# Attention scores as float32 products in quarters of the array instead of packed halves

## The chip, the cores and the metric

The kernel runs on one core of one Trainium2 chip. The metric is the device time of one execution in microseconds. Three executions of the kernel before gave 1820.46, 1821.09 and 1821.55 us, median 1821.09 us. The engines are TensorE (PE in the rows, its weight loads PEld), VectorE (DVE), ScalarE (ACT), GpSimd (POOL) and the DMA queues, here those that SyncE fills (SP).

## What is computed

Input is `x` of shape (8, 512, 128). Four layers follow, each as `x = x + layernorm(layer(layernorm(x)))`: a linear attention with a feed-forward part (stage `pf` in the kernel), a rotary attention with a causal mask and a choice of two of eight experts (`rope` and `mo`), a context attention (`ctx`), and a gated expert network (`sw`). The change touches the two softmax attentions. Both have 16 heads of 8 channels and 512 tokens in each of 8 samples. The rotary one:

```python
q_in = rope(x)                                  # keys from it too, values from x
q, k, v = (inp @ W.T + b).reshape(B, S, 16, 8)
scores = einsum('bqhd,bkhd->bhqk', q, k) * 8 ** -0.5
scores = where(causal, scores, -inf)
out = einsum('bhqk,bkhd->bqhd', softmax(scores), v) @ Wo.T + bo
```

The context attention has no mask and adds one term for all heads, from 16 further channels:

```python
ctx = X @ We.T                                  # 16 channels a token
scores = einsum('bhqd,bhkd->bhqk', Q, K) * 8 ** -0.5 + 0.1 * einsum('bqe,bke->bqk', ctx, ctx)[:, None]
```

So a score of the rotary layer sums 8 channels, one of the context layer 24.

## The kernel before

`attention_layer` holds both attentions (`causal` tells them apart). A sample's 16 heads go in 4 groups of `GH = 4`; the queries of a head are 4 tiles of 128 tokens. A softmax needs the largest score of each query first, then the exponentials, and it is computed in two products:

- **Scores** (`score`, L1310, into `s` banks): queries in the rows of the result, keys along 512 columns. VectorE takes the largest of each row (`largest`, L1176, `nm`), negated. In the rotary layer a tile needs only the keys up to its own (128, 256, 384 or 512 columns), and a bf16 product adds the mask (L1313).
- **By key** (`scores_by_key`, L1657, into `st` banks): keys in the rows, queries along the columns, with the negated largest score as one more channel, the guard. ScalarE writes `exp` of it to `probs` (L1554, 1024 columns at a time); in the rotary layer GpSimd zeroes the future (L1419).
- **Values** (`weigh_values`, L1673, into `out`): for each key block the four heads of a group go to the four column quarters of the array, each as a 128 x 32 float32 product.

The operands of the first two are stacks of channels, `qst` and `kst`, in fp32r. Each channel stands in them as a high and a low half, in three rows (high by low, low by high, high by high), which makes 24 rows in the rotary layer and 72 in the context layer, in a stack of 96; the guard takes rows 96 and 97. A product by the full array then gives the float32 result in one pass. The halves are made by GpSimd (`halves_of`, L1106 and L1108, `halves_of_context`), written to DRAM by `store_halves` (L1034) and loaded per group by `load_stack` (L1047, L1050). The guard is cut in two halves on VectorE (`cut_guard`, L1185, L1188), transposed (L1193) and goes to DRAM and back (L1054, L1062) for each group.

The loop of a layer runs over rounds `b` (samples) and 32 steps `h` in each, eight to a group. In a round TensorE scores the group two ahead, makes the products by key of the present group and the values of the group behind (in two lots, at the steps 3 and 7 of a group). Into the steps are put the side products of the samples before and after: turning the tokens, the projections q, k, v and c, turning the output (`o0`, `o1`, `oT`) and projecting it (`wo`). The score banks are a ring, `SR = 3`: `vacated` makes a product wait for whoever reads what the bank held three uses earlier, for a score the reduction (semaphore `s_used`). In the context layer side products use the ring too; in the rotary layer they have a bank of their own (`side`). Two pairs of `st` banks alternate. ScalarE copies the output bank after every second group (L1561), twice a sample.

The first group's scores of sample 0 are made by the stage before, in banks lent by it (`pf_dve`; `mo_side` and `mo_lp`). The stage `pf` uses parts of the attention buffers as its own memory (`room`).

## Time and profile before

| what | us |
|---|---|
| median of three executions | 1821.09 |
| profiled execution, its own time | 1818.61 |
| its span, first to last instruction | 1816.9 |
| TensorE busy | 1527.4 (84%) |
| VectorE busy | 1249.6 (69%) |
| ScalarE busy | 1027.1 (57%) |
| GpSimd busy | 793.7 (44%) |
| first layer (`pf`) | about 0 to 370 |
| rotary attention loop | about 373 to 756 |
| experts (`mo`) | about 760 to 930 |
| context attention loop | about 934 to 1401 |
| last layer (`sw`) | to the end |

Busy time of an engine over the whole span mixes stages with different limits, so the table of stretches below is read stage by stage. A record of a TensorE product is longer than the time that the array streams, as the next one starts before it ends; where a group of products follows without a gap, the difference of starts is what one costs. "x8" behind a row of a timeline counts records.

### The profile page before, as it was taken

What the parts mean: (1) busy time and instruction counts of PE and PEld (TensorE: products, weight loads), DVE (VectorE), ACT (ScalarE), POOL (GpSimd) and SP (SyncE); (2) the same over time, 40 slices, a digit from 0 to 9 for tenths busy, and PEclk for the clock granted to TensorE, in tenths of its full rate; (3) what the DMA queues carried; (4) which work ended last, traced back from release to release, by engine and by line L of the source; (5) the groups of instructions that cost most, each with busy time, mean ns of one, the idle gap of its engine ahead of it and who ended that gap; (6) DMA issues with size and microseconds to landing.
All of it is one profiled execution on the core that took longest, in us unless ns stands there. A gap on an engine that the chain in (4) does not pass through costs nothing. (4 is left out here: it accounts for less than half of the span.)

```text
span 1816.9 us, 26731 instructions
## 1 busy us (share of the span) xinstructions
PE 1527.4 (84%) x8757; PEld 964.7 (53%) x8757; DVE 1249.6 (69%) x3212; ACT 1027.1 (57%) x1749; POOL 793.7 (44%) x902
## 2 busy tenths in 40 slices
PE   3788888689999999588769999999997686999980
PEld 1444555466666666343335545555553565777770
DVE  1656667467777777267777778777882574888875
ACT  2444555335666655424636677677675554777762
POOL 2244534435555544324741111222001576688875
PEclk8888989759999999788868999999998698999995
DMA  6800000212222221000244444443530022344415
GB/s 214 278 1 1 1 1 1 61 60 78 69 74 72 70 73 35 4 14 1 72 107 122 109 110 121 120 120 92 131 72 1 32 68 90 117 126 136 126 55 139
DMA packets 96201, 144.30 MB, mean 79 GB/s; under 512 B 31266, under 2 KB 59939, under 8 KB 91952
## 3 DMA queue, kind: packets, MB, share of 16 engines
q1 hardware_dynamic: 91072, 134.11, 26.5%
q0 software_dynamic: 4992, 8.48, 1.4%
q8 instruction: 71, 1.16, 0.3%
q14 instruction: 66, 0.54, 0.1%
HBM read 104.19 MB, written 57.48 MB: 89 GB/s over the span
## 5 line engine op out<-in xcount | busy, mean ns | idle before, releaser
L1176 DVE TENSOR_REDUCE ctx_nm<-ctx_s 128x1 f32<-128x512 f32 x496 | 320.0, 681 | 87.4 <-PE ctx_s L1310 86.6
L1176 DVE TENSOR_REDUCE rope_nm<-rope_s 128x1 f32<-128x128 f32 x496 | 223.5, 481 | 83.0 <-PE rope_s L1313 80.7
L1554 ACT ACTIVATE rope_probs<-rope_st 128x1024 f32<-128x1024 f32 (+1 forms) x256 | 172.2, 702 | 139.1 <-PE rope_st L1657 137.9
L1554 ACT ACTIVATE ctx_probs<-ctx_st 128x1024 f32<-128x1024 f32 x192 | 190.3, 1023 | 87.6 <-PE ctx_st L1657 84.1
L1310 PE MATMUL ctx_s<-att_kst,att_qst 96*128 96x512 f32 x496 | 210.9, 459 | 19.4 <-DVE ctx_nm L1176 8.4
L1310 PE MATMUL rope_s<-att_kst,att_qst 96*128 96x128 f32 x496 | 179.0, 392 | 8.8 <-PEq L120 5.5
L1657 PE MATMUL ctx_st<-att_qst,att_kst 98*128 98x512 f32 x512 | 164.7, 404 | 2.4 <-ACT ctx_probs L1554 1.5
L1419 POOL TENSOR_SCALAR_AFFINE_SELECT rope_probs<-rope_probs 128x256 f32<-128x256 f32 x256 | 98.1, 408 | 156.1 <-ACT rope_probs L1554 155.6
L1310 PEld LDWEIGHTS ctx_s<-att_kst,att_qst 96*128 96x128 f32 x496 | 95.8, 193 | 127.3 <-DVE ctx_nm L1176 51.0
L1657 PE MATMUL rope_st<-att_qst,att_kst 98*128 98x512 f32 (+3 forms) x512 | 141.2, 360 | 3.9 <-ACT rope_probs L1554 3.9
L2930 DVE TENSOR_TENSOR sw_hl<-sw_hf,sw_hh 128x512 fp32r<-128x512 f32 x124 | 128.5, 1037 | 0.1
L2924 DVE TENSOR_TENSOR sw_hf<-sw_silu,sw_u 128x512 f32<-128x512 f32 x124 | 84.7, 683 | 62.8 <-ACT sw_silu L2682 58.1
L2682 ACT ACTIVATE sw_silu<-sw_g 128x512 f32<-128x512 f32 x124 | 74.3, 599 | 92.4 <-PE sw_g L110 91.9
L1673 PE MATMUL ctx_out<-ctx_probs,att_vaug 128*32 128x512 f32 x768 | 122.5, 598 | 0.0
L1310 PEld LDWEIGHTS rope_s<-att_kst,att_qst 96*128 96x128 f32 x496 | 100.5, 203 | 37.3 <-issue 22.3
L2782 POOL DMA_INDIRECT sw_ys<-sw_yo,sw_xin x92 | 104.2, 1132 | 29.1 <-issue 24.0
L1313 PE MATMUL rope_s<-rope_maskb,rope_identb 128*128 128x128 bf16 x496 | 116.5, 239 | 0.0
L1657 PEld LDWEIGHTS ctx_st<-att_qst,att_kst 98*128 98x128 f32 x512 | 98.3, 194 | 24.4 <-issue 4.6
L1657 PEld LDWEIGHTS rope_st<-att_qst,att_kst 98*128 98x128 f32 x512 | 92.1, 200 | 14.6 <-ACT rope_probs L1554 5.9
L2761 POOL TENSOR_TENSOR sw_wl<-sw_raw,sw_wh 128x1536 fp32r<-128x1536 f32 x24 | 84.1, 3503 | 34.8 <-ACT sw_wh L2660 34.8
L1673 PE MATMUL rope_out<-rope_probs,att_vaug 128*32 128x512 f32 (+3 forms) x1024 | 84.1, 448 | 3.0 <-POOL rope_probs L1419 3.0
L2688 ACT ACTIVATE sw_hh<-sw_hf 128x512 fp32r<-128x512 f32 x124 | 77.3, 624 | 5.5 <-DVE sw_hf L2924 5.5
(429 smaller groups left out, 3467.1 us busy)
## 6 DMA issues: line engine op xcount, KB each, us to landing
sw_raw<-in_L_ffn_all SPq DMA_DIRECT2D x24, 768.0 KB, 4.4
sw_xs<-in_pad SPq DMA_DIRECT2D x65, 260.0 KB, 9.5
rope_halves<-att_qk SPq DMA_DIRECT2D x24, 512.0 KB
ctx_halves<-att_qk SPq DMA_DIRECT2D x24, 512.0 KB, 5.7
att_qst<-ctx_contexts SPq DMA_DIRECT2D x32, 384.0 KB
att_kst<-ctx_contexts SPq DMA_DIRECT2D x32, 384.0 KB
att_qst<-rope_halves SPq DMA_DIRECT2D x32, 192.0 KB
att_kst<-rope_halves SPq DMA_DIRECT2D x32, 192.0 KB
```

The lines of the kernel that those rows point to most:

```text
L1176: nc.vector.tensor_reduce(nm[:, g, j * T + t:j * T + t + 1], bank("s", b, n)[:, 0:keys], AXX, ALU.max, negate=True).then_inc(s_used, 1)
L1310: last = nc.tensor.matmul(out[:, 0:keys], qst[0:KS, g, j, t * P:(t + 1) * P], kst[0:KS, g, j, 0:keys], start=True, stop=not causal)
L1313: last = nc.tensor.matmul(out[:, keys - P:keys], identb[:], maskb[:], start=False, stop=True)
L1419: last = nc.gpsimd.affine_select(blocks, blocks, [[0, 2], [1, P]], compare_op=ALU.is_ge, fill=0.0, base=0, channel_multiplier=-1)
L1554: nc.scalar.activation(prob(n // GH % 2, n % GH)[:, u * units[0]:u * units[0] + units[u]], st_bank[u][:, 0:units[u]], ACT.Exp, scale=SCALE ...
L1657: last = nc.tensor.matmul(st_bank[u][:, lo:lo + width[c]], kst[:, g, j, c * P:(c + 1) * P], qst[:, g, j, S - width[c]:S], start=True, stop ...
L1673: last = nc.tensor.matmul(o_bank[32 * j:32 * j + 32, S - width[c]:S], vaug[g // 2][:, s, c, j, :], prob(s, j)[:, at(c):at(c) + width[c]], ...
L2688: nc.scalar.activation(hh[m % RING][:], hf[m % 3][:], ACT.Copy).then_inc(hh_ready, 1)
L2761: nc.gpsimd.tensor_tensor(wl[s % WR][:], raw[s % 2][:], wh[s % WR][:].bitcast(F32), ALU.subtract).then_inc(wl_ready, 1)
L2782: nc.gpsimd.indirect_dma_start(ys[:, :], bass.IndirectOffsetOnAxis(ap=where_to, axis=0), yo[j % YR][:, t, :], None, bounds_check=2 * B * S ...
L2924: nc.vector.tensor_tensor(hf[m % 3][:], silu[m % 2][:], u_bank[m % 2][:], ALU.mult).then_inc(hf_ready, 1)
L2930: nc.vector.tensor_tensor(hl[m % RING][:], hf[m % 3][:], hh[m % RING][:].bitcast(F32), ALU.subtract).then_inc(hl_ready, 1)
```

## The change

Each head's channels are now stored once, as plain float32, and the four heads of a group stand in the four quarters of the partitions (`QUARTER = 32`): rows 0 to 7 of a quarter are the channels, in the context layer rows 8 to 23 the context, and row 31 (`GUARD`) the guard, as one float32 number against ones in `kst`. A product takes 31 rows (scores) or 32 (by key) of a quarter of the array's rows and all 128 columns. All code for halves goes. The scores of a pair (two heads, one query tile) and the products by key of the other two heads (one key block) make a step:

```diff
-            def score(b, g, j, t):
-                n = (g * GH + j) * T + t
+            def scores(b, pair):
 ...
-                vacated("s", b, n)
-                keys = P * (t + 1) if causal else S
-                out = bank("s", b, n)
-                last = nc.tensor.matmul(out[:, 0:keys], qst[0:KS, g, j, t * P:(t + 1) * P], kst[0:KS, g, j, 0:keys],
-                                        start=True, stop=not causal)
-                if causal:
-                    last = nc.tensor.matmul(out[:, keys - P:keys], identb[:], maskb[:], start=False, stop=True)
-                last.then_inc(s_ready, 1)
+                two = (2 * pair, 2 * pair + 1)
+                g = pair // PAIRS
+                for n in two:
+                    vacated("s", b, n)
+                    j, t = scored(n % (GH * T))
+                    keys = P * (t + 1) if causal else S
+                    rows = slice(QUARTER * j, QUARTER * j + GUARD)
+                    last = nc.tensor.matmul(bank("s", b, n)[:, 0:keys], qst[rows, b % 2, g, t * P:(t + 1) * P], kst[rows, b % 2, g, 0:keys],
+                                            start=True, stop=not causal)
+                    if not causal:
+                        last.then_inc(s_ready, 1)
+            def hide_future(b, pair):
+                for n in (2 * pair, 2 * pair + 1):
+                    keys = P * (scored(n % (GH * T))[1] + 1)
+                    nc.tensor.matmul(bank("s", b, n)[:, keys - P:keys], identb[:], maskb[:], start=False, stop=True).then_inc(s_ready, 1)
```

`scored` gives the heads 2 and 3 in even steps and 0 and 1 in odd ones; the products by key take the others:

```diff
-            def scores_by_key(b, g, j, u):
+            def scores_by_key(b, g, i):
+                m = (b * NG + g) * PAIRS + i
+                if i == 0:
+                    pe.wait_ge(m_loaded[g % 2], (b * NG // 2 + g // 2 + 1) * 16)
+                if m >= 2:
+                    pe.wait_ge(p_ready, m - 1)
+                c, half = i // 2, i % 2
+                for k in range(2):
+                    rows = slice(QUARTER * (2 * half + k), QUARTER * (2 * half + k + 1))
+                    last = nc.tensor.matmul(st_bank[half][:, k, 0:width[c]], kst[rows, b % 2, g, c * P:(c + 1) * P],
+                                            qst[rows, b % 2, g, S - width[c]:S], start=True, stop=True)
 ...
                     ahead, behind = group(b, g + 2), group(b, g - 1)
                     if within(ahead[0]) and not lead(ahead):
-                        score(*ahead, j, 2 * u)
+                        scores(ahead[0], ahead[1] * PAIRS + i)
                     now = keys_step(b, h)
                     if now:
-                        scores_by_key(now[0], now[1] // 8, j, u)
-                    if within(ahead[0]) and not lead(ahead):
-                        score(*ahead, j, 2 * u + 1)
+                        scores_by_key(*now)
+                    if within(ahead[0]) and not lead(ahead) and causal:
+                        hide_future(ahead[0], ahead[1] * PAIRS + i)
```

In the rotary layer the columns of a step now fall over the group, for scores and products by key alike: 512, 512, 384, 384, 256, 256, 128, 128. The banks stay eight: three score banks, four by key (the rotary side bank goes there, and its side products into the ring), one for the output. Storing and loading are by sample:

```diff
-            def load_stack(b, g, side_tile, side):
 ...
+            def load_stacks(b):
+                if causal and b == 0:
+                    sp.wait_ge(init, 4)
+                sp.wait_ge(stored, (b + 1) * NS)
+                for side, st in enumerate((qst, kst)):
+                    src = parts[b, side].rearrange("(d g j) t -> j d g t", g=NG, j=GH)
+                    for j in range(GH):
+                        row = QUARTER * j
+                        sp.dma_start(st[row:row + DH, b % 2], src[j]).then_inc(stacks_loaded[b % 2], 16)
+                        if not causal:
+                            sp.dma_start(st[row + DH:row + DH + CE, b % 2], contexts[b, side].unsqueeze(1).broadcast_to([CE, NG, S])).then_inc(stacks_loaded[b % 2], 16)
```

VectorE transposes `nm` itself (`turn_guard`), with no cut. GpSimd clears both stacks and sets the value buffers once at the start of `pf` (`prepare`) instead of in its rounds and at the loop's start, and `pf` gets buffers of its own in place of `room`.

TensorE's order in the context loop, before, with the number of the score bank and of the by-key bank:

```order
L1657 MATMUL ctx_st1<-att_qst,att_kst 128x512 x2
L1310 MATMUL ctx_s1<-att_kst,att_qst 128x512
L1287 MATMUL ctx_s2<-att_yT,att_wk 128x512
L1310 MATMUL ctx_s0<-att_kst,att_qst 128x512
L1657 MATMUL ctx_st0<-att_qst,att_kst 128x512 x2
L1310 MATMUL ctx_s1<-att_kst,att_qst 128x512
L1310 MATMUL ctx_s2<-att_kst,att_qst 128x512
L1657 MATMUL ctx_st1<-att_qst,att_kst 128x512 x2
L1310 MATMUL ctx_s0<-att_kst,att_qst 128x512
```

The same loop after the change:

```order
L1280 MATMUL ctx_s1<-att_kst,att_qst 128x512
L1280 MATMUL ctx_s2<-att_kst,att_qst 128x512
L1600 MATMUL ctx_st1<-att_qst,att_kst 128x512 x2
L1280 MATMUL ctx_s0<-att_kst,att_qst 128x512
L1280 MATMUL ctx_s1<-att_kst,att_qst 128x512
L1600 MATMUL ctx_st0<-att_qst,att_kst 128x512 x2
L1572 MATMUL ctx_s2<-ident,mo_we 128x128 x4
L1280 MATMUL ctx_s0<-att_kst,att_qst 128x512
L1280 MATMUL ctx_s1<-att_kst,att_qst 128x512
```

One score stood on either side of the two products by key; now both stand ahead of them, and the second takes the bank that the first one of the step before had (`s1` after `s1`, two rows apart).

TensorE's order in the rotary loop, before:

```order
L1310 MATMUL rope_s1<-att_kst,att_qst 128x128
L1313 MATMUL rope_s1<-rope_maskb,rope_identb 128x128
L1657 MATMUL rope_st0<-att_qst,att_kst 128x512
L1657 MATMUL rope_st0<-att_qst,att_kst 128x384
L1657 MATMUL rope_st0<-att_qst,att_kst 128x128
L1310 MATMUL rope_s2<-att_kst,att_qst 128x256
L1313 MATMUL rope_s2<-rope_maskb,rope_identb 128x128
```

And after the change:

```order
L1280 MATMUL rope_s1<-att_kst,att_qst 128x256
L1280 MATMUL rope_s2<-att_kst,att_qst 128x256
L1600 MATMUL rope_st0<-att_qst,att_kst 128x256 x2
L1288 MATMUL rope_s1<-rope_maskb,rope_identb 128x128
L1288 MATMUL rope_s2<-rope_maskb,rope_identb 128x128
L1280 MATMUL rope_s0<-att_kst,att_qst 128x256
L1280 MATMUL rope_s1<-att_kst,att_qst 128x256
L1600 MATMUL rope_st1<-att_qst,att_kst 128x256 x2
```

The mask, on all rows and columns of the array, stood right behind its score; now both masks of a step stand behind the step's four products.

## Rows read from the trace of the kernel before

**Rows 1.** Table of stretches: from:to, length, busy us by engine, PEclk, DMA

```profile
365.00:420.00 55.00, 49.18 (x256) 34.67 (x259) 35.15 (x91) 19.91 (x32) 23.92 (x45) 0.68 0.24 74
...
420.00:735.00 315.00, 306.46 (x2437) 210.75 (x2436) 243.05 (x695) 191.29 (x322) 164.69 (x320) 1.00 0.21 64
985.00:1370.00 385.00, 374.25 (x1979) 201.81 (x1978) 308.78 (x689) 272.08 (x335) 63.28 (x85) 1.00 0.44 111
907.00:927.00 20.00, 10.97 (x16) 4.53 (x16) 15.49 (x41) 6.58 (x17) 11.56 (x10) 0.50 0.62 120
```

**Rows 2.** Timeline of ScalarE: start us, length us, the copies of the output bank

```profile
514.40 0.60 ACT L1561 ACTIVATE rope_oe<-rope_out 128x512 f32<-128x512 f32 x1 [0.74 <-PE rope_out L1673]
...
561.48 0.60 ACT L1561 ACTIVATE rope_oe<-rope_out 128x512 f32<-128x512 f32 x1 [0.73 <-PE rope_out L1673]
...
1104.70 0.60 ACT L1561 ACTIVATE mo_we<-ctx_out 128x512 f32<-128x512 f32 x1 [1.09 <-PE ctx_out L1673]
...
1162.28 0.60 ACT L1561 ACTIVATE mo_we<-ctx_out 128x512 f32<-128x512 f32 x1 [1.10 <-PE ctx_out L1673]
```

**Rows 3.** Timeline of TensorE in the context loop, scores and values

```profile
1108.99 0.39 PE L1310 MATMUL ctx_s<-att_kst,att_qst 96*128 96x512 f32 x1
1109.31 1.92 PE L1673 MATMUL ctx_out<-ctx_probs,att_vaug 128*32 128x512 f32 x16
...
1111.98 0.63 PE L1310 MATMUL ctx_s<-att_kst,att_qst 96*128 96x512 f32 x2
```

**Rows 4.** Timeline of TensorE in the first stage, two products in column quarters

```profile
51.53 0.62 PE L316 MATMUL pf_act<-pf_sqq,pf_hsel 128*32 128x512 f32 x1
51.54 0.62 PE L317 MATMUL pf_act<-pf_sqk,pf_hsel 128*32 128x512 f32 x1
51.98 0.59 PE L316 MATMUL pf_act<-pf_sqq,pf_hsel 128*32 128x512 f32 x1
51.99 0.59 PE L317 MATMUL pf_act<-pf_sqk,pf_hsel 128*32 128x512 f32 x1
```

**Rows 5.** Timeline of TensorE in the rotary loop, around values

```profile
560.39 0.23 PE L1313 MATMUL rope_s<-rope_maskb,rope_identb 128*128 128x128 bf16 x1
560.55 0.86 PE L1673 MATMUL rope_out<-rope_probs,att_vaug 128*32 128x256 f32 x16
561.34 0.33 PE L1310 MATMUL rope_s<-att_kst,att_qst 96*128 96x128 f32 x1
```

**Rows 6.** Timeline of the context loop, hand-overs between TensorE and VectorE

```profile
1107.49 0.65 DVE L1176 TENSOR_REDUCE ctx_nm<-ctx_s 128x1 f32<-128x512 f32 x1
...
1108.19 0.50 PE L1310 MATMUL ctx_s<-att_kst,att_qst 96*128 96x512 f32 x1 [0.19 <-DVE ctx_nm L1176]
...
1111.17 0.50 PE L1310 MATMUL ctx_s<-att_kst,att_qst 96*128 96x512 f32 x1
...
1111.70 4.39 DVE L1176 TENSOR_REDUCE ctx_nm<-ctx_s 128x1 f32<-128x512 f32 x7 [1.03 <-PE ctx_s L1310]
```

**Rows 7.** Groups by shape, rotary loop: xcount, busy us, mean ns, idle before

```profile
L1176 DVE TENSOR_REDUCE rope_nm<-rope_s 128x1 f32<-128x512 f32 x109 | 72.8, 668 | 0.0
...
L1176 DVE TENSOR_REDUCE rope_nm<-rope_s 128x1 f32<-128x128 f32 x108 | 30.7, 284 | 31.4 <-PE rope_s L1313 31.1
```

**Rows 8.** Timeline of TensorE in the context loop, two side products

```profile
1099.78 1.13 PE L1644 MATMUL ctx_s<-ctx_wo,ctx_oT 128*128 128x128 f32 x8
...
1121.57 0.63 PE L1628 MATMUL ctx_s<-ident,mo_we 128*128 128x128 f32 x4 [0.28 <-DVE ctx_nm L1176]
```

**Rows 9.** Timeline of TensorE in the expert stage, first group's scores

```profile
912.63 0.80 PE L1310 MATMUL mo_side<-att_kst,att_qst 96*128 96x512 f32 x1 [0.19 <-DVE ctx_nm L1176]
...
914.21 0.79 PE L1310 MATMUL mo_side<-att_kst,att_qst 96*128 96x512 f32 x1 [0.19 <-DVE ctx_nm L1176]
```

**Rows 10.** GpSimd in the first stage: timeline row, then a group by shape

```profile
26.57 1.26 POOL L487 TENSOR_TENSOR att_qk<-pf_y,pf_bo 128x512 f32<-128x512 f32 x1 [18.07 <-DMA pf_be<-in_L_attn_be]
...
L1122 POOL MEMSET att_kst<- 96x2048 f32 x4 | 7.2, 1804 | 0.0
```

More of the change, by code:

```diff
@@ L246, in _ @@
                 sp.dma_start(dst[:], src).then_inc(signal, 16)
-            behind.store_halves(0)
-            behind.fill_stacks()
+            behind.store_parts(0)
+            behind.load_stacks(0)
+            behind.store_parts(1)
+            behind.load_stacks(1)
             behind.store_guard(0, 0)
@@ L461, in _ @@
                     behind.project_values(1)
-                    for n in range(GH * T):
-                        behind.score(0, 0, n // T, n % T)
+                    for pair in range(GH * T // 2):
+                        behind.scores(0, pair)
+                        behind.hide_future(0, pair)
         @block.gpsimd
@@ L515, in _ @@
             behind.set_half()
+            behind.prepare()
             for b in rounds:
@@ L530, in _ @@
                     behind.turn(1, 0)
-                    pool.wait_ge(r_ready, B)
-                    behind.halves_of(0, 0)
-                    behind.halves_of(0, 1)
                 if within(f2):
@@ L727, in _ @@
                     if b == B + 2 + n // (GH * T // 2):
-                        behind.largest(0, 0, n // T, n % T)
-            for step in range(3):
-                behind.cut_guard(0, 0, step)
+                        behind.largest(0, n)
+            behind.turn_guard(0, 0)
         @block.scalar
@@ L994, in attention_layer, with scored @@
         rounds = range(-1, B + 1)
-        lent_bank, ring, side, lent = [], [], [], []
+        def scored(n):
+            i, k = n // 2, n % 2
+            return 2 * (1 - i % 2) + k, T - 1 - i // 2 if causal else i // 2
+        lent_bank, ring, lent = [], [], []
         for c in range(LEAD):
@@ L1004, in attention_layer @@
             for h in range(STEPS):
-                to, tg = group(b, h // 8 + 2)
+                to, tg = group(b, h // PAIRS + 2)
                 if within(to) and not lead((to, tg)):
-                    ring += [("s", to, tg * GH * T + h % 8 * 2 + k) for k in range(2)]
+                    ring += [("s", to, tg * GH * T + h % PAIRS * 2 + k) for k in range(2)]
                 for name, step in AT.items():
@@ L1010, in attention_layer @@
                     if step == h and within(own) and (name in OUTPUTS or own >= LEAD):
-                        (side if SIDE else ring).append((name, own, 0))
-        spot = {use: (uses, n) for uses in (ring, side, lent) for n, use in enumerate(uses)}
-        assert len(spot) == len(ring) + len(side) + len(lent) == B * (GH * NG * T + len(AT))
+                        ring.append((name, own, 0))
+        spot = {use: (uses, n) for uses in (ring, lent) for n, use in enumerate(uses)}
+        assert len(spot) == len(ring) + len(lent) == B * (GH * NG * T + len(AT))
         def banks(name, b, k=0):
             uses, n = spot[name, b, k]
-            return uses, n, lent_bank if uses is lent else side_bank if uses is side else s_bank
+            return uses, n, lent_bank if uses is lent else s_bank
         def bank(name, b, k=0):
@@ L1023, in keys_step @@
         def keys_step(b, h):
[L1025 to L1029 removed]
+            if b * STEPS + h < PAIRS:
+                return (0, 0, b * STEPS + h + PAIRS) if -PAIRS <= b * STEPS + h < 0 else None
+            return (b, h // PAIRS, h % PAIRS) if within(b) else None
+        s_bank = []
         def on_sync(sp):
[L1032 to L1050 removed]
@@ L1324, in attention_layer @@
         s_bank += [ps(f"s{k}", 512) for k in range(SR)]
-        side_bank += [ps(f"side{k}", 512) for k in range(SIDE)]
-        st_bank = [ps("st0", 1024), ps("st1", 512 if causal else 1024)]
+        st_bank = [main.enter_context(nc.psum_tensor(layer + f"st{k}", [P, 2, 512], F32)) for k in range(2)]
         o_bank = ps("out", 512)
@@ L1445, in _ @@
                     now = keys_step(b, h)
-                    if causal and now and h % 2 == 1:
-                        hide_future(now[0], now[1] // 2)
+                    if causal and now:
+                        hide_future(*now)
                     if within(c) and c >= LEAD:
@@ L1452, in _ @@
                             turn(c, h - TURN)
-                        for k, name in enumerate("qk"):
-                            if h == AT[name] + 1:
-                                halves_of(c, k)
-                        if not causal and h == AT["c"] + 1:
-                            halves_of_context(c, 0)
-                            halves_of_context(c, 1)
                     if within(a):
@@ L1589, in _ @@
                     if now:
-                        exponentials(now[0], now[1] // 2, h % 2)
+                        exponentials(*now)
                     if within(c) and c >= LEAD:
@@ L1622, in _ @@
         def _(pe):
-            vacated, turn_tokens, turn_rotated, project, project_values, project_context, score = on_tensor(pe)
+            vacated, turn_tokens, turn_rotated, project, project_values, project_context, scores, hide_future = on_tensor(pe)
             def turn_out(a, hf):
@@ L2092, in _ @@
                             project_ahead(c, (b - first - 2) * T + t)
-                    for n in SCORED.get((b, t), []):
-                        next_layer.score(0, 0, n // T, n % T)
+                    for pair in SCORED.get((b, t), []):
+                        next_layer.scores(0, pair)
                     if ahead and t == 0:
```

328 lines of the change are left out of this document (118 added, 210 removed).

## The prediction

> **What bounds the kernel now.** I first read the table of stretches [rows 1]. In the loop of the rotary attention (420 to 735 us) TensorE is busy 306.5 of 315 us, in the loop of the context attention (985 to 1370 us) 374 of 385 us, both at a granted clock of 1.00, which is 2.4 GHz. VectorE follows with 243 and 309 us. So TensorE sets both loops, VectorE is close behind in the second, and everything that the change takes from GpSimd and the DMA queues lies under cover there. The copy of the output bank by ScalarE comes twice a sample, so every second one gives the time of a sample: 561.48 - 514.40 = 47.1 us (rotary), 1162.28 - 1104.70 = 57.6 us (context) [rows 2]. These two periods are what the change alters. A steady sample has all its scoring; groups are scored two ahead and the first one by the stage before, so each loop scores 31 groups of 4 to a sample, 7.75 samples.
>
> **Products.** A packed product of 512 columns is one record, and dense ones start 0.63 - 0.39 = 0.24, in longer runs 0.23 us apart [rows 3]. A float32 product is two records: 16 records for four heads and two key blocks take 1.92 us, of which 0.16 is the tail of the last; so 2 x 4 products take 1.76 us, and four products in four column quarters run in 0.86 us, the time of one [rows 3]. That they overlap across quarters, though each has two records, shows in the first stage: two products of L316 and L317 begin 0.01 us apart, and their second records 0.45 us later, again 0.01 apart [rows 4]. The queue does not wait for the second record of one quarter before it starts another. The trace has columns in quarters, not rows. I take rows in quarters to overlap as well (nearest row), and keep a serial array, 4 x 0.86 = 3.44 us, as the other end.
> A step of the context loop was 4 x 0.23 = 0.93 us of streaming; it becomes 0.86 us if all four products start together. That saving, 0.07 x 32 = 2.2 us a sample, is all there is to win on the array.
>
> **Changes of tiling.** Between the full array and the quarters of the value products the stream stops: the mask product of 560.39 streams until 560.46 (0.23 less the tail of 0.16) and the value products begin at 560.55; they end at 561.25, and the scores begin at 561.34 [rows 5]. That is 0.09 us each way. Behind values of 512 columns (end 1111.07) the score of 1111.17 has a record of 0.50 instead of 0.39 [rows 3, 6], 0.2 in all. I take 0.14. The trace has no change from row quarters to full; bounds 0 and 0.3.
> In the context loop this adds two changes for each of nine side products a sample, in the rotary loop two for each step, since the mask stays a product on the full array.
>
> **The wait that decides.** The ring of scores keeps 3 banks. A step asks for two of them; the second one is the bank of the first product of the step before. Its wait stands ahead of both products by key in TensorE's queue. Hand-overs: a reduction that ends at 1108.14 lets a product start at 1108.19 (0.05), whose record is 0.50 instead of 0.39 long, since its weights were not loaded ahead (0.10) [rows 6]; a product that ends at 1111.67 is reduced from 1111.70 (0.04), and seven reductions in a row take 4.39 us, 0.62 apart [rows 6], each 0.67 long [rows 7]. From the start of a first product to the start of the next step's second one: 0.86 + 0.16 + 0.04 + 0.67 + 0.05 + 0.10 = 1.9 us. Before, the same round trip was 0.23 + 0.16 + 0.04 + 0.67 + 0.15 = 1.25 us and had three dense products of 0.23 and the products by key to hide in. The longer product, not the number of reductions, makes the difference.
> Half a group of the context loop, from a free array at 0: step 0 starts all four at 0. Step 1: first at 0.86 (its quarter is then free), second at 1.9, by key at 1.9. Step 2: first at 1.9 + 0.86 = 2.76, second at 3.1 (its bank's reduction is the third in VectorE's row), by key 3.1. Step 3: first 4.0, second 2.76 + 1.9 = 4.65, by key 4.65, end 5.5. Then the value products: 0.14 + 1.72 + 0.14. Sum 7.5 us, eight times a sample: 60.0. The nine side products: three of 512 columns at 0.86, two of eight records at 1.13 - 0.16 = 0.97 less overlap, 0.9 [rows 8], four turns of four records, 0.63 - 0.16 = 0.47 with the start, 0.44 [rows 8], together 6.1, and 9 x 0.28 = 2.5 for tiling. **Context sample 68.7 us, +11.1.**
> Half a group of the rotary loop: columns fall 512, 512, 384, 384, and the scores are only ready behind the mask. From one mask to the next step's second product: 0.23 (mask record) + 0.04 + reduction + 0.05 + 0.10 = 0.42 + 0.67 for 512 columns, 0.42 + 0.28 for 128 [rows 7]; I put 0.55 and 0.42 between. First half: mask at 0.86 + 0.14 = 1.0; then +1.09 + 1.0 = 3.1; +1.09 + 0.78 = 4.95; +0.97 + 0.78 = 6.7; two masks, tiling and values (0.86 + 0.64) give 8.6. Second half (256, 256, 128, 128): 0.57, +0.84 + 0.57 = 1.98, +0.84 + 0.36 = 3.2, +0.70 + 0.36 = 4.25, and 1.0 behind them: 5.25. A group 13.85, a sample 55.4. Side products 2 x 0.86 + 2 x 0.9 + 5 x 0.44 = 5.7, whose tiling is already counted. **Rotary sample 61.1 us, +14.0.**
> Over 7.75 samples: +86 and +108.
>
> **Fronts.** The first group of the context loop is scored inside the expert stage, at a granted clock of 0.50 (1.2 GHz) [rows 1] and with two lent banks: a pair each 914.21 - 912.63 = 1.58 us [rows 9]. Now a product is 1.71 us, and the second bank comes back after 1.71 + 0.25 + 0.04 + 0.62 + 0.68 + 0.15 = 3.4 us; eight pairs +14.6 us, of which other VectorE work hides perhaps a third: +10. The rotary front has falling columns and masks: +8. The first round of each loop still runs at the low clock (0.68 on the mean of 365 to 420 us [rows 1]), where the longer products cost double: +5.
> **Under cover.** GpSimd loses the halves and the clearing; in both loops it waits more than it works. It now clears the stacks at its start, four memsets of 1.8 us (96 x 2048 took 1.80 [rows 10]) and the value buffers, some 2.3 us, until about 16.5 us; it sat idle 18.07 us up to 26.57 for a load [rows 10], and TensorE's first projection waits for a load as well: +1 (0 to +5). Two cuts a group (VectorE, 0.3 us) go, on an engine that waits here. A sample's stacks are loaded at once, behind one guard and ahead of the next in the queue, with fewer bytes; there is most of a group (14 us and more) for it. 0, at most +2 a sample if a guard is late. The first stage no longer borrows memory: 0 to -5.
> **Sum** against the profiled execution, 1818.6 us (span 1816.9 and 1.7 around it; the median of the runs is 1821.1): 1818.6 + 86 + 108 + 10 + 8 + 5 + 1 = 2036.6, say **2036 us**.
>
> **Rivals.**
> 1, the clock falls. At 2.4 GHz TensorE was busy 97% of the loops; 907 to 927 us shows it busy 11.0 of 20 us at 1.2 GHz [rows 1]. In the new rotary loop a quarter works 4 x (4.28 + 2.13 + 0.8) + 5.7 = 34.5 of 61 us, which lies between those rows. At 1.2 GHz each group pays 4.28 + 2.13 us again and side products 5: +30.6 a sample, +237. Half the time: 2155; all of it: 2273. With the context loop as well (5.2 us a half group, +46 a sample) 2630.
> 2, row quarters overlap in part. As a mechanism: the second record of one product must start before the next product may, so four products take 5 records of 0.43, 2.15 us a step. Context: 32 x 2.15 + 13.8 + 2.2 + 8.6 = 93.4, +36 a sample; rotary: 4 x (2.5 x 4.28 + 3.0) + 15.3 = 70 or a little more, +25. Time 1818.6 + 473 + 24 = 2315. Fully serial (3.44): +77 and +49, 2820. The rows of L316 and L317 speak against it [rows 4]. The Trainium skill, TensorE: Matmul & The Clock Gate, section "What overlaps and what doesn't", says that products start and end in program order; read strictly, with two records to a product, that is this case.
> 3, the other side: the ring does not bind. If the second bank is free when asked for (because quarters run ahead of each other and VectorE has caught up during values and side products), the array alone sets the pace: context 32 x 0.86 + 13.8 + 2.2 + 8.6 = 52.1 (-5.5), rotary 4 x (4.28 + 8 x 0.38) + 8.5 + 1.1 + 5.7 = 44.6 (-2.5): -62 + 24, 1781 us. It decides where the round trip of 1.9 us is under 1.3; half the stall gives about 1910.
> The same page, section "Measured speedup vs the span model", gives 3.07 times, not 4, for four row tiles of 512 columns. An estimate by it: 1.12 us a step, some 65 us more in the context loop and 40 in the rotary one, about 2140. No row here shows it, and the sum goes without it.
>
> **Numbers.** Forecast as worked out, 1950 to 2100: 0.55. Clock: 0.18. Partial or no overlap: 0.12. The ring binding half or not at all: 0.15, of which 0.09 is faster than before and 0.02 the same. Range 1900 to 2290: it leaves out the fast end and the serial one. A measurement of this kernel tells 0.2% from no change: faster 0.09, same 0.02, slower 0.89.
>
> **What would show it.** Right: in the context loop records of four products of 512 columns begin together only behind value or side products; otherwise the second score starts 1.9 us after the first of the step before, its weight load released by the reduction; the output copies are 68 and 61 us apart; VectorE idles more than before. Wrong: if four products take 2 us or more with no wait (rival 2), if the granted clock is under 1.00 in a loop (rival 1), or if the waits of the scores for reductions stay as short as in [rows 6] and the periods fall (rival 3). If both loops keep their periods, the round trip was mis-sized.

## The result: 2038.6 us, 12% slower than before

The changed kernel takes a median of 2038.63 us (2029.98 to 2045.13, four executions); the kernel before took 1820.78 us (1815.92 to 1821.55, four, one more than at first). The ratio is 1.12, with a 95% interval of 1.115 to 1.125. The profiled execution took 2035.4 us, against 2036.6 of the sum. The sum hides two errors of opposite sign, though. By stage, a loop being counted from the weight load of its first product by key to the start of its last product of values (us):

| stretch | before | after | change | forecast |
|---|---|---|---|---|
| up to the rotary loop | 373.4 | 375.9 | +2.5 | +8 (front) +1 (start), 0 to -5 (own memory) |
| rotary loop | 380.5 | 509.2 | +128.7 | +108, and most of 5 |
| experts | 180.0 | 182.3 | +2.3 | +10 |
| context loop | 459.8 | 545.6 | +85.8 | +86, and the rest of 5 |
| last layer | 423.1 | 420.7 | -2.4 | 0 |

The profile page of the changed kernel, busy time by engine and two groups of its section 5:

```profile
PE 1772.0 (87%) x10805; PEld 905.7 (45%) x10805; DVE 1235.8 (61%) x3086; ACT 1042.5 (51%) x1749; POOL 696.1 (34%) x801
...
L1153 DVE TENSOR_REDUCE ctx_nm<-ctx_s 128x1 f32<-128x512 f32 x496 | 320.4, 684 | 169.9 <-PE ctx_s L1280 168.8
...
L1280 PEld LDWEIGHTS ctx_s<-att_kst,att_qst 31*128 31x128 f32 x992 | 136.3, 188 | 213.1 <-DVE ctx_nm L1153 103.7
```

The 496 reductions cost what they did before (320.0 us then). What grew is the waiting on both sides of them: VectorE now idles 169.9 us ahead of them (87.4 on the page of before), and the weight loads of the scores wait 103.7 us for reductions (51.0 before). GpSimd fell from 794 to 696 us busy and the DMA queues moved 92.6 MB instead of 144.3. In the two loops no gain from either shows. In the experts' stage one does, as the fronts below tell: there TensorE had stood waiting for the stacks to be loaded.

The table of stretches (from:to, length, busy us by engine, granted clock, DMA) answers to [rows 1]:

```profile
350.00:425.00 75.00, 66.00 (x234) 30.66 (x236) 30.48 (x81) 13.19 (x21) 11.97 (x22) 0.52 0.08 19
700.00:720.00 20.00, 19.95 (x132) 8.63 (x128) 9.41 (x32) 7.65 (x13) 7.48 (x14) 0.66 0.18 28
430.00:850.00 420.00, 414.49 (x3319) 189.22 (x3318) 230.33 (x641) 200.20 (x319) 148.57 (x296) 0.97 0.08 18
1120.00:1580.00 460.00, 458.71 (x2858) 168.19 (x2859) 306.85 (x632) 277.29 (x334) 26.06 (x45) 1.00 0.15 29
```

TensorE shows as busy for 99.7% of the context loop, more than the 97% before, though it gets through fewer products in a microsecond: with four products under way, a quarter that waits is hidden behind the others' records. VectorE's share fell from 80% to 67% there. Busy share alone would have named the array as the limit. The copies of the output bank by ScalarE, answering to [rows 2], give the periods:

```profile
507.68 0.60 ACT L1505 ACTIVATE rope_oe<-rope_out 128x512 f32<-128x512 f32 x1 [0.62 <-PE rope_out L1613]
...
569.70 0.60 ACT L1505 ACTIVATE rope_oe<-rope_out 128x512 f32<-128x512 f32 x1 [0.62 <-PE rope_out L1613]
...
1300.28 0.60 ACT L1505 ACTIVATE mo_we<-ctx_out 128x512 f32<-128x512 f32 x1 [0.24 <-PE ctx_out L1613]
...
1368.83 0.60 ACT L1505 ACTIVATE mo_we<-ctx_out 128x512 f32<-128x512 f32 x1 [0.23 <-PE ctx_out L1613]
```

Context 68.55 us a sample (forecast 68.7). Rotary 62.0 us here, with one fall of the clock in it, and 60.5 where the clock stayed at 1.00 (forecast 61.1).

Half a group of the context loop on TensorE, answering to [rows 3, 6]; each product is two records, and L1280 are scores, L1600 products by key:

```profile
1344.66 0.70 PE L1280 MATMUL ctx_s<-att_kst,att_qst 31*128 31x512 f32 x2
1344.67 0.70 PE L1600 MATMUL ctx_st<-att_qst,att_kst 32*128 32x512 f32 x2
1345.19 0.59 PE L1280 MATMUL ctx_s<-att_kst,att_qst 31*128 31x512 f32 x2
1345.21 0.59 PE L1600 MATMUL ctx_st<-att_qst,att_kst 32*128 32x512 f32 x2
1345.64 1.62 PE L1280 MATMUL ctx_s<-att_kst,att_qst 31*128 31x512 f32 x3
1346.57 0.70 PE L1600 MATMUL ctx_st<-att_qst,att_kst 32*128 32x512 f32 x2
...
1347.53 0.92 PE L1280 MATMUL ctx_s<-att_kst,att_qst 31*128 31x512 f32 x2
1347.77 0.70 PE L1600 MATMUL ctx_st<-att_qst,att_kst 32*128 32x512 f32 x2
...
1348.73 1.30 PE L1280 MATMUL ctx_s<-att_kst,att_qst 31*128 31x512 f32 x3
1349.34 0.70 PE L1600 MATMUL ctx_st<-att_qst,att_kst 32*128 32x512 f32 x2
...
1350.40 0.64 PE L1613 MATMUL ctx_out<-ctx_probs,att_vaug 128*32 128x512 f32 x4
```

And its weight loads and VectorE:

```profile
1346.56 0.18 PEld L1280 LDWEIGHTS ctx_s<-att_kst,att_qst 31*128 31x128 f32 x1 [0.74 <-DVE ctx_nm L1153]
...
1349.33 0.18 PEld L1280 LDWEIGHTS ctx_s<-att_kst,att_qst 31*128 31x128 f32 x1 [0.41 <-DVE ctx_nm L1153]
```

```profile
1345.82 2.59 DVE L1153 TENSOR_REDUCE ctx_nm<-ctx_s 128x1 f32<-128x512 f32 x4 [2.01 <-PE ctx_s L1280]
```

At 1344.66 four products start together, their second records 0.53 us on, again together: row quarters overlap. The first score of the next step starts at 1345.64, and for nearly a microsecond it is alone in the array. The second score's weights are released by a reduction at 1346.56, 1.90 us after 1344.66, and both products by key go with it, at 1346.57: they needed nothing, they stood behind.

### The profile page after: what moved, and what is told of

Same layout as the page of the kernel before. It is cut to its first block and busy times, and to the rows that moved or that the text cites. A ratio compares the mean times of both kernels' runs of the same rounds, so it can differ in the third digit from the quotient of the medians.

```text
span 2033.7 us, 30332 instructions
## 1 busy us (share of the span) xinstructions
PE 1772.0 (87%) x10805; PEld 905.7 (45%) x10805; DVE 1235.8 (61%) x3086; ACT 1042.5 (51%) x1749; POOL 696.1 (34%) x801
## 5 line engine op out<-in xcount | busy, mean ns | idle before, releaser
L1153 DVE TENSOR_REDUCE ctx_nm<-ctx_s 128x1 f32<-128x512 f32 x496 | 320.4, 684 | 169.9 <-PE ctx_s L1280 168.8
L1280 PE MATMUL ctx_s<-att_kst,att_qst 31*128 31x512 f32 x992 | 367.5, 644 | 8.9 <-PEq L120 7.3
L1153 DVE TENSOR_REDUCE rope_nm<-rope_s 128x1 f32<-128x512 f32 (+1 forms) x496 | 220.7, 484 | 224.6 <-PE rope_s L1288 224.6
L1280 PE MATMUL rope_s<-att_kst,att_qst 31*128 31x512 f32 (+1 forms) x992 | 320.2, 521 | 10.0 <-PEq L120 4.2
L1498 ACT ACTIVATE rope_probs<-rope_st 128x1024 f32<-128x1024 f32 (+3 forms) x256 | 178.4, 703 | 259.0 <-PE rope_st L1600 258.4
L1600 PE MATMUL ctx_st<-att_qst,att_kst 32*128 32x512 f32 x1024 | 287.3, 648 | 2.9 <-ACT ctx_probs L1498 2.9
L1280 PEld LDWEIGHTS ctx_s<-att_kst,att_qst 31*128 31x128 f32 x992 | 136.3, 188 | 213.1 <-DVE ctx_nm L1153 103.7
L1600 PE MATMUL rope_st<-att_qst,att_kst 32*128 32x512 f32 (+3 forms) x1024 | 218.9, 514 | 3.7 <-ACT rope_probs L1498 3.7
L1280 PEld LDWEIGHTS rope_s<-att_kst,att_qst 31*128 31x128 f32 x992 | 134.4, 196 | 114.0 <-DVE rope_nm L1153 68.5
L1498 ACT ACTIVATE Y<-ctx_st 128x1024 f32<-128x1024 f32 x64 | 65.4, 1022 | 39.0 <-PE ctx_st L1600 39.0
L1600 PEld LDWEIGHTS rope_st<-att_qst,att_kst 32*128 32x128 f32 x1024 | 79.9, 194 | 10.5 <-ACT rope_probs L1498 7.7
```

The lines of the kernel that those rows point to most:

```text
L1153: nc.vector.tensor_reduce(nm[:, g, col:col + 1], bank("s", b, n)[:, 0:keys], AXX, ALU.max, negate=True).then_inc(s_used, 1)
L1280: last = nc.tensor.matmul(bank("s", b, n)[:, 0:keys], qst[rows, b % 2, g, t * P:(t + 1) * P], kst[rows, b % 2, g, 0:keys], start=True, sto ...
L1498: nc.scalar.activation(prob(g % 2, half)[:, :, at(c):at(c) + width[c]], st_bank[half][:, :, 0:width[c]], ACT.Exp, scale=SCALE if causal el ...
L1600: last = nc.tensor.matmul(st_bank[half][:, k, 0:width[c]], kst[rows, b % 2, g, c * P:(c + 1) * P], qst[rows, b % 2, g, S - width[c]:S], st ...
```

## Experiments

Unless said otherwise an edit is to the changed kernel, and a period is that of a steady sample between copies of the output bank. Times of the experiments are of one execution each, but for before_no_mask. Four runs (short_reduce, second_behind, one_quarter, one_pass) share a chip, on which the kernel before took 1815.4 us; four (both, pair_order, no_mask_product, one_pass_twice) share another, where it took 1836.4; before_no_mask ran on a third (1837.3). The difference between chips shows in the last layer, the same code in all kernels: 420 to 423 us on the first, 437 to 442 on the others. So the loops are compared, not the totals.

| kernel | rotary | context | clock, from within each loop | time |
|---|---|---|---|---|
| before | 47.1 | 57.6 | 1.00, 1.00 | 1820.8 |
| after | 60.5 to 65.2 | 68.5 | 0.97, 1.00 | 2038.6 |
| short_reduce | 53.8 to 55.4 | 61.3 | 0.99, 1.00 | 1909.9 |
| second_behind | 60.2 to 61.8 | 67.7 | 0.98, 1.00 | 2021.2 |
| both | 53.5 | 59.2 | 1.00, 1.00 | 1907.0 |
| pair_order (edit of before) | 48.8 to 51.9 | 59.6 to 61.5 | 0.98, 0.98 | 1873.2 |
| no_mask_product | 50.7 | 68.5 | 1.00, 1.00 | 1957.9 |
| one_quarter | 178 to 183 | 249 to 253 | 0.52, 0.54 | 4354.7 |
| one_pass | 54 to 58 | 59 to 63 | 0.74, 0.80 | 1920.1 |
| one_pass_twice | 59 to 64 | 61 to 67 | 0.79, 0.90 | 1999.3 |
| before_no_mask (edit of before) | 45.3 to 47.0 | 57.6 | 0.98, 1.00 | 1819.9 |

**Does the reduction sit in the path?** short_reduce:

```diff
             def largest(b, n):
 ...
-                keys = P * (t + 1) if causal else S
+                keys = P
```

> The kernel after, but the largest score is taken over the first 128 keys only, in both attentions (so the guard is not the true maximum; everything else is computed). Ring theory (the second score of a step waits for the reduction of the first score of the step before): a reduction of 0.28 us instead of 0.67 makes the round trip 1.5 instead of 1.9 us, a half group of the context loop 4.7 instead of 5.5 us, its sample 62 instead of 68.5 us; the rotary sample 56 instead of 61 us; about 1950 us in all. Array theory (products in row quarters and changes of tiling alone set the pace): VectorE only idles more, the samples stay at 68.5 and 61 us and the time at 2038 us.

The array has the same work, and 129 us went. In the context loop the 32 steps of a sample became 7.2 us shorter in all. An array that sets the pace would have kept its periods. Each loop gave 60 us, where I had worked out 50 and 39; the side with the ring stands.

**Who stands behind the waiting score?** second_behind issues one score ahead of the products by key and the other behind them:

```diff
 ...
-                        scores(ahead[0], ahead[1] * PAIRS + i)
+                        scores(ahead[0], ahead[1] * PAIRS + i, (0,))
                     now = keys_step(b, h)
                     if now:
                         scores_by_key(*now)
+                    if within(ahead[0]) and not lead(ahead):
+                        scores(ahead[0], ahead[1] * PAIRS + i, (1,))
```

> The kernel after, with the second score of each step issued behind the two products by key instead of ahead of them; all is computed. Ring theory: the products by key no longer stand behind the wait, but three banks and a reduction row of 0.62 us each still hold the scores: a half group of the context loop 5.2 instead of 5.5 us, sample 66 us, the rotary loop unchanged (its mask comes behind all four), about 2020 us. If the queue position alone makes the stall (head of line), the context sample falls to the array's own 52 to 56 us, 1920 us. If neither matters: 2038 us.

0.9 us of a context sample, where 2.5 were expected. That the time is near the expected 2020 is partly luck: the context loop gave 7 us instead of 20, and the rotary loop, which I had put as unchanged, gave 9. What is queued behind the wait is not the main cost, as long as the trip is this long: this kernel has the long products in the order of before, and its context sample is still 10.1 us above the 57.6. That kills the cheap repair.

**What is left when both go?** both has the two edits together.

> The changed kernel with both earlier edits together: VectorE reduces only 128 of the 512 keys (this leaves out most of the maximum), and the second score of a step stands behind the two products by key. Theory (the round trip of the score banks sets the pace): the trip is 0.86 + 0.16 + 0.04 + 0.29 + 0.05 + 0.10 = 1.50 us and nothing but the second score waits for it, so the array sets the context loop, with what the by-key banks add (product, result, exp of 1.02, product again: 2.2 us for two steps, which binds in four steps of a half group by some 0.4 us): 54 to 56 us a sample against 61.3 with the short reduction alone and 68.5 in the changed kernel. Rotary 52 to 53 (53.8 alone), since the mask keeps its place. Time about 1865. Rival (the remainder of the loop is not the ring but products that overlap less than taken, or changes of tiling): the order brings nothing here, 61 and 54 us a sample, about 1905.

Context 59.2, between the two numbers and nearer the rival's 61: with a short reduction the order brings 2.1 us, where I had expected 5 to 7. (The time is level with short_reduce, since this chip's last layer is 16 us slower.) What holds it up shows on TensorE and ScalarE of this kernel, in half a group that starts at 1306.24:

```profile
1306.24 0.70 PE L1600 MATMUL ctx_st<-att_qst,att_kst 32*128 32x512 f32 x2
...
1307.20 0.59 PE L1600 MATMUL ctx_st<-att_qst,att_kst 32*128 32x512 f32 x1
...
1308.53 0.69 PE L1600 MATMUL ctx_st<-att_qst,att_kst 32*128 32x512 f32 x1
...
1309.44 0.69 PE L1600 MATMUL ctx_st<-att_qst,att_kst 32*128 32x512 f32 x1
```

```profile
1307.45 1.94 ACT L1498 ACTIVATE ctx_probs<-ctx_st 128x1024 f32<-128x1024 f32 x2 [1.90 <-PE ctx_st L1600]
```

The third step's products by key start 2.29 us after the first's, when the first exp is done (1307.45 + 1.02 = 1308.47), and the fourth's at the end of the second. The two pairs of by-key banks are the next ring. So even with a reduction that looks at a quarter of the keys, and with the better order, a sample of this loop takes 59.2 us, more than the 57.6 before.

**Order or length?** pair_order takes the kernel before, with its packed products, and puts both scores ahead:

```diff
                         score(*ahead, j, 2 * u)
+                        score(*ahead, j, 2 * u + 1)
                     now = keys_step(b, h)
                     if now:
                         scores_by_key(now[0], now[1] // 8, j, u)
-                    if within(ahead[0]) and not lead(ahead):
-                        score(*ahead, j, 2 * u + 1)
```

> The kernel before with one edit: both scores of a step stand ahead of the two products by key, as in the changed kernel, while products stay packed on the full array at 0.23 us. Theory (the length of the float32 product makes the round trip long; order alone costs little): the trip is 1.25 us against a step of 0.93 + 0.23 to the second score of the next step, so at most 0.1 us a step, context 58 to 60 us a sample (57.6 before), rotary 47 to 49 (47.1): 1820 to 1850 us. Rival (the wait ahead of the products by key is what costs, whatever the product's length): most of the +86 us of the context loop comes back here, 1880 to 1900.

At the full clock +2.0 us a context sample and +1.7 a rotary one, of the +10.9 and +13.4 of the change. So order alone is a small part. In the context loop length is the large one; the rotary loop has the mask besides. The time lies above my range: with the new gaps the granted clock is 0.50 for 3.4 us in each of four context samples, and for 6.8 and 3.4 us in two rotary ones (0.98 over both loops), another 2 us or so where it is, and the chip's last layer adds its 17.

**The mask.** no_mask_product leaves out the mask product, so the maximum is over unmasked scores:

```diff
                     last = nc.tensor.matmul(bank("s", b, n)[:, 0:keys], ...
-                                            start=True, stop=not causal)
-                    if not causal:
-                        last.then_inc(s_ready, 1)
+                                            start=True, stop=True)
+                    last.then_inc(s_ready, 1)
 ...
             def hide_future(b, pair):
 ...
+                pass
```

> The changed kernel without the mask product on TensorE in the rotary layer (the maximum is taken over the unmasked scores of a tile's keys; GpSimd still zeroes the future). Theory: the score's result is ready 0.86 us after its start instead of behind the step's four products and the mask, and two changes of tiling a step go: rotary sample about 50 us against 60.5 to 62, 7.75 samples and the front, some 90 us: about 1950. Context sample unchanged at 68.5. Rival (the rotary loop's excess over the forecast comes from the granted clock, which dips with the array's load, and not from the mask): at most 57 us a sample, about 2005, with a lower granted clock.

50.7 us, as the theory said. The rotary loop took 408.5 us, 101 less. The mask behind the four products costs 9.8 us a sample. It makes the result of a score ready late and changes the tiling twice a step; no run tells the two apart. The kernel before pays for its mask too, 1.8 us (47.1 against 45.3 in before_no_mask, below). So of the 13.4 us by which a rotary sample grew, 8.0 are the mask in its new place, and 5.4 (50.7 against 45.3) would be there without any mask. The clock is 1.00 again, and 60.5 us is what the changed kernel's samples take at 1.00 too, so its dips there are not what made the sample grow.

**Do quarters overlap?** one_quarter sends all products through the first quarter of the rows:

```diff
-                    rows = slice(QUARTER * j, QUARTER * j + GUARD)
+                    rows = slice(0, GUARD)
 ...
-                    rows = slice(QUARTER * (2 * half + k), QUARTER * (2 * half + k + 1))
+                    rows = slice(0, QUARTER)
```

> The kernel after, with all products of scores and by key on the first quarter of rows (so every head of a group gets the first head's scores; the count and size of all products is as before). If the row quarters overlap fully in the kernel after, four products now take 3.4 us instead of 0.86 us: context sample about 134 us, rotary sample about 100 us, some 2850 us in all. If they overlap only in part there (four products in 2.15 us), the loss is smaller, some 2550 us. If they do not overlap there: 2038 us.

TensorE, then the stretch of the context loop:

```profile
3000.33 3.62 PE L1600 MATMUL ctx_st<-att_qst,att_kst 32*128 32x512 f32 x4
3003.75 3.62 PE L1280 MATMUL ctx_s<-att_kst,att_qst 31*128 31x512 f32 x4
3007.16 3.62 PE L1600 MATMUL ctx_st<-att_qst,att_kst 32*128 32x512 f32 x4
```

```profile
2500.00:4000.00 1500.00, 1473.47 (x2653) 547.37 (x2652) 299.30 (x660) 284.32 (x367) 57.13 (x73) 0.54 0.04 8
```

Two products take 3.41 us, so four take 6.83, and 32 steps 219 of the 249 us. In the changed kernel four take 0.98 (1344.66 to 1345.64). Without any overlap there the edit would have changed nothing. The excess over every expectation is the clock, which no theory had: at the granted 0.54, nearly always 1.2 GHz, a product takes 1.71 us instead of 0.86, although the engine is busy 98% of the time.

**A shorter product.** one_pass declares the stacks as fp32r, so a product is one record and less exact:

```diff
-        self.kst, self.qst = sb("kst", [P, 2, NG, S]), sb("qst", [P, 2, NG, S])
+        self.kst, self.qst = sb("kst", [P, 2, NG, S], F32R), sb("qst", [P, 2, NG, S], F32R)
 ...
```

> The kernel after, with the stacks read as fp32r, so that each product in a quarter is one short record instead of two long ones (channels and guard lose their low bits; nothing else changes, same order, same waits, same ring). Ring theory: a product of 0.22 us cuts the round trip from 1.9 to 1.25 us: context sample 47 to 50 us, then set by VectorE, rotary sample 48 us, about 1770 us in all. If the order of the pair or the changes of tiling made the loss, the samples stay near 68 and 61 us.

```profile
430.00:800.00 370.00, 351.78 (x2323) 163.27 (x2324) 218.06 (x618) 192.38 (x307) 144.16 (x286) 0.74 0.09 18
1060.00:1400.00 340.00, 304.43 (x1607) 107.65 (x1605) 242.00 (x520) 224.42 (x280) 22.10 (x37) 0.80 0.20 39
```

118 us faster, and 150 slower than the ring's number. By half groups of the context loop (from values to values, the same places of a sample): where the clock is 1.00, 7.78, 6.6 and 6.3 us instead of 9.81, 8.88 and 7.59; where it is 0.50, 9.9 instead of 8.84. The shorter trip does help at full speed, and the array, now with gaps, runs at 1.2 GHz some 40% of the context stretch.

An estimate of how much it would help: four half groups in a row held 1.00 and took 27.6 us where the changed kernel takes 35.7; at that ratio a context sample would take 53 us, against some 61 measured and the 47 to 50 expected. Most of the miss in the context loop would then be the clock, and a few us something else.

**Would more work pay by holding the clock?** one_pass_twice issues each of these products twice:

```diff
+                    for again in (True, False):
+                        last = nc.tensor.matmul(bank("s", b, n)[:, 0:keys], ...
+                                                start=True, stop=again or not causal)
 ...
+                    for _ in range(2):
+                        last = nc.tensor.matmul(st_bank[half][:, k, 0:width[c]], ...
```

> The one-pass kernel (stacks as fp32r, 1920.1 us, granted clock 0.807) with each of the four products of a step issued twice into its bank, the second over the first: 4 products of two passes in a quarter each, 0.46 us a step at the full clock instead of 0.23, still below the 0.86 of float32. Theory (the one-pass kernel loses its gain because the array works too little and the granted clock falls): the clock rises to 0.88 or more and the time does not grow in spite of twice the products, 1870 to 1920. Rival (the clock has another cause, or was not what cost the time): the clock stays about 0.8 and each step pays for the added products where they are not hidden, 1940 to 1970.

Neither number was met; the rival is the nearer one. The clock rose (0.74 to 0.79, 0.80 to 0.90), and yet the rotary loop grew by 46 us and the context loop by 11 (the other 20 of the 79 us are the chip's last layer). At the full clock, half groups at the same places went from 6.6 to 7.3 us (context) and from 7.66 to 8.50 and 5.74 to 6.17 (rotary): a product longer by some 0.2 us costs 0.4 to 0.9 in four steps even at full speed, as a longer trip would, and the clock gives back less than that. So the clock can't be bought back in this way. How much of one_pass's miss is the clock rests on the estimate above, as no run held it at 1.00 through a loop with short products in quarters.

**A version that beats both kernels.** before_no_mask takes the mask product out of the kernel before:

```diff
                 last = nc.tensor.matmul(out[:, 0:keys], ...
-                                        start=True, stop=not causal)
-                if causal:
-                    last = nc.tensor.matmul(out[:, keys - P:keys], identb[:], maskb[:], start=False, stop=True)
+                                        start=True, stop=True)
                 last.then_inc(s_ready, 1)
```

> The kernel before (packed halves on the full array) without the mask product of the rotary layer: the largest score of a row is taken over all keys of the tile's columns, future ones too, and GpSimd still zeroes the future after exp. Any guard at or above the largest allowed score leaves the softmax as it is, so the output stays that of the reference as long as no future score exceeds the allowed ones by so much that exp underflows. It asks whether a version beats both kernels. Theory (TensorE sets the rotary loop, busy 97%): 64 products of 128 columns of bf16 go from a sample, 0.06 to 0.10 us each on the array, 4 to 6 us, until VectorE (243 of 315 us busy, 36 us a sample) or the ring holds: rotary sample 42 to 44 us instead of 47.1, 7.75 samples: 25 to 40 us less, about 1785 where the kernel before takes 1818. Rival (the score ring and VectorE already set the pace of that loop): 46 to 47 us a sample, at most 8 us less. Second rival (the array, now less busy, loses the granted clock in the rotary loop): under 1.00 there, and no gain or a loss.

1819.89 us (four executions) against 1837.27 (seven) on the same chip, ratio 0.990 (0.987 to 0.994): 1% less, small but clear of the scatter. The stretch of the rotary loop, to be read beside [rows 1]:

```profile
420.00:735.00 315.00, 291.46 (x2040) 188.93 (x2036) 242.77 (x694) 195.45 (x329) 167.58 (x327) 0.98 0.20 61
```

The loop takes 368.5 us instead of 380.5, which is 12 of the 17 us. A sample takes 45.3 us at the full clock, between the 42 to 44 of the theory and the 46 to 47 of the first rival, and 47.0 or more where the clock now dips: the second rival eats part of the gain. The price is a guard that can be too high where a future score towers over the allowed ones.

## Why the prediction was right, and where it was not

**The round trip** was right, each start to within 0.12 us. From a free array the forecast put the starts of scores at 0, 0.86, 1.9, 2.76, 3.1, 4.0 and 4.65 us; the rows show 0, 0.98, 1.90, 2.87, 3.11, 4.07 and 4.68, and 7.59 us from values to values where I had 7.5. short_reduce shows that the reduction lies in that trip. pair_order (new order, short products: +2.0 us) and second_behind (old order, long products: +10.1 us) show that in the context loop the float32 length and not the order makes it bind. A fourth score bank, the direct test of the ring, was not run.

**Rows in quarters** overlap, as taken. Rival 2 is out. The Trainium skill, TensorE: Matmul & The Clock Gate, section "The mechanism", under "What overlaps and what doesn't", has products start and end in program order. Product by product the trace of after agrees: the first score of a step starts at 1347.53, ahead of the products by key at 1347.77, and its second record starts at 1347.97, ahead of theirs at 1348.30. Record by record it doesn't: that second record at 1347.97 starts behind the first records of later products at 1347.77. So the strict reading in rival 2 is the wrong one. The estimate of 1.12 us for four products, from the 3.07 times of the same page of the Trainium skill, section "Measured speedup vs the span model", is above what they take here, 0.98 us.

**Changes of tiling.** In short_reduce the array ends a step's streaming at 1201.83 + 0.43 = 1202.26 and a product on all rows starts at 1202.36: 0.10 us, where I took 0.14 and bounds of 0 and 0.3.

**The rotary sample** came out at 60.5 us for 61.1, with the mask's new place as its largest part, as no_mask_product and before_no_mask show. But the loop grew by 16 us more than the 108 + 5. Seven periods (from the first copy of the output bank in each sample to that of the next) make 107.7 of its 128.7, where 7 x 14.0 = 98 was forecast; the dips of the clock (periods of 62 to 65 us instead of 60.5) are most of the difference. The remaining 21 are the first round and the loop's tail, for which three quarters of a sample and the 5 us give 15. That is rival 1 in small: it was put as half or all of a loop, and came as single stretches of 3 to 14 us (the longest lies in the row of 700 to 720 us above), and as a longer cold start: 0.52 over 350 to 425 us, where the kernel before has 0.71 over the same stretch.

**The fronts** came out almost as forecast; what the sum missed is a gain ahead of them. In the experts' stage the first group, from its first score to the end of its last reduction, takes 26.3 us (1034.46 to 1060.77), against 17.4 before (909.48 to 926.86): 8.9 more, for the 10 of my sum. A pair of scores at 1.2 GHz takes 2.85 us instead of the 3.4 of my working, and no other work hides a third of it:

```profile
1043.03 1.22 PE L1280 MATMUL mo_side<-att_kst,att_qst 31*128 31x512 f32 x1 [0.19 <-DVE ctx_nm L1153]
...
1045.88 1.22 PE L1280 MATMUL mo_side<-att_kst,att_qst 31*128 31x512 f32 x1 [0.18 <-DVE ctx_nm L1153]
```

In the first stage the same stretch takes 22.0 us for 14.2, which is 7.8 for my 8. The stages grew by 4.8 us only, as their first scores start earlier. In the experts' stage it is 6.1 us earlier, and 4.6 of them stand in front of that score. The first row is of before, the second of after:

```profile
909.48 0.79 PE L1310 MATMUL mo_side<-att_kst,att_qst 96*128 96x512 f32 x1 [9.48 <-DMA att_kst<-ctx_contexts]
...
1034.46 1.22 PE L1280 MATMUL mo_side<-att_kst,att_qst 31*128 31x512 f32 x1 [4.88 <-DMA att_kst<-ctx_contexts]
```

TensorE waits 4.9 us for the stacks there instead of 9.5. The three kernels that cut their operands in halves wait 9.0 to 9.5 us at this place, the changed one and its seven edits 4.1 to 5.7. So the making, storing and loading of halves, which my working put under cover by a look at the loops, was not under cover here. No run tells the three apart, nor from the loading by sample that came with the change. In the first stage the first score starts at 350.0 instead of 354.1 us, but over the edits of the changed kernel it starts anywhere from 350 to 355, so what is gained there is not clear of scatter; my working had 0 to -5 for it, and the sum took 0.

So 16 us too few in one loop stood against 14 too many in the two stages ahead of the loops, and 2 in the last layer. That they cancel is luck: the total is closer than its parts.

## What to carry to other kernels

Packing products into quarters keeps the array's throughput but multiplies the latency of each result; with a ring of a few banks count the whole trip (product, result, reader, hand-over) and divide by the steps it spans, before counting what the array does. A busy share near 100% on an engine that runs several products at once says nothing on whether it is the limit: shorten the suspected reader and see whether the period moves. And a product that only prepares another engine's clean-up, as the mask here, may be left out altogether.

## What the runs showed of the hardware that I had not expected

In one_quarter, where nearly all products of the two loops go through one quarter of the rows, TensorE was busy 98 to 100% of the time and was granted 0.52 and 0.54 over 1000 and 1500 us. Short products in four quarters got 0.74 to 0.80, while float32 ones in four quarters held 1.00 in the context loop. The last layer, the same code in all kernels, took 420 to 423 us on one chip and 437 to 442 on two others; what makes the difference is open. The loops hardly differ by chip, as far as it shows: no kernel was profiled on two of them, but the context sample of no_mask_product, on the second chip, takes the same 68.55 us as that of the changed kernel.
